# A mixture-of-experts block on one core: W2 loaded ahead of the last rows of W1, slot tables built among the first tiles, merged rank sums, eight products for the W2 row sums, no unread products, and the last ten tile words loaded by SyncE

## The reference

```python
x = x + xattn(ctx, ctx, layernorm(x), Wk, Wv, bv, Wq, bq, Wo, bo)   # 16 x 256 tokens of 128, 64 keys for each batch
t = layernorm(x)                                                    # 4096 tokens
p = softmax(t @ Wr + br)                                            # 8 experts
probs, idx = top_k(p, 2); probs = probs / probs.sum(-1)
h = layernorm(relu(t @ W1[e] + b1[e])) * g1[e] + be1[e]             # 128 -> 512, for each expert
y = layernorm(relu(h @ W2[e] + b2[e])) * g2[e] + be2[e]             # 512 -> 128
out = x + sum over the token's two experts of gate * y
```

## Time and profile before

| | |
|---|---|
| runs, median (range) | 316.07 us (314.22 to 317.29) |
| profiled execution, and its span | 314.07 us, 312.4 us |
| TensorE matmul, weight load | 251.5 us (81%), 196.5 us (63%) |
| VectorE, ScalarE, GpSimd | 227.6 (73%), 208.3 (67%), 189.3 us (61%) |
| mean granted TensorE clock | 0.885 of full |
| DMA | 34.46 MB, mean 110 GB/s |

### The profile page before, as it was taken

The page is one execution under the profiler, slowest core; times in us unless marked ns, Lnnn a source line. Parts: engine busy times, 40 slices in busy tenths (PEclk is TensorE's granted clock), DMA queues, the critical chain, the costliest instruction groups (busy, mean ns, idle before and its releaser), DMA issues.

```text
span 312.4 us, 8770 instructions
## 1 busy us (share of the span) xinstructions
PE 251.5 (81%) x2605; PEld 196.5 (63%) x2605; DVE 227.6 (73%) x1091; ACT 208.3 (67%) x795; POOL 189.3 (61%) x298
## 2 busy tenths in 40 slices
PE   2998629795929292746997998999999999899895
PEld 2465427454728171314896887798989987899531
DVE  1687918560359366738796778798989898899875
ACT  2557517734636294672796769698989898799920
POOL 8403545572634536364746786768888887788750
PEclk9998958877857667585998999999999999999999
DMA  6995672210411131243533123223232459551347
GB/s 183 342 286 173 199 238 62 76 43 28 135 35 60 59 104 52 59 100 87 113 65 75 47 62 81 61 68 70 72 72 45 129 131 196 138 137 46 96 146 241
DMA packets 48667, 34.46 MB, mean 110 GB/s; under 512 B 26871, under 2 KB 42743, under 8 KB 48620
## 3 DMA queue, kind: packets, MB, share of 16 engines
q1 hardware_dynamic: 38972, 22.80, 27.5%
q0 software_dynamic: 6592, 9.00, 9.9%
q10 hardware_dynamic: 3056, 2.11, 2.2%
HBM read 15.11 MB, written 12.02 MB: 87 GB/s over the span
## 4 chain that ended last, share of the span: by engine, by line
PE 35%; DVE 32%; another core or an unknown queue 14%; ACT 10%; issue 6%; DVEq 1%; DMA 1%; ACTq 0%
PE bank L720 20%; PE bank L724 13%; DVE kq L1884 5%; DVE cxT L1900 3%; DVE cx L1915 3%; DVE st L1905 2%; DVE hl L1884 2%; DVE w2f L1651 2%; ACT ex L1179 2%; ACT xt L1202 1%; DVE rs L1924 1%; ACT w1l L1221 1%; DMA wr<-in_L_ffn_Wr 1%; DVEq L1896 1%
## 5 line engine op out<-in xcount | busy, mean ns | idle before, releaser
L664 POOL DMA_INDIRECT slot_rows<-pay,pos x64 | 64.8, 1013 | 62.8 <-DVE pay L1757 45.7
L724 PE MATMUL bank<-w2h,kq 128*128 x384 | 59.1, 222 | 4.7 <-DVE cxT L1900 3.8
L720 PE MATMUL bank<-kb_room,w1h 128*128 128x128 f16 x568 | 57.4, 223 | 1.3 <-issue 0.9
L720 PE MATMUL bank<-kb_room,w1l 128*128 128x128 f16 x284 | 52.9, 223 | 0.5 <-issue 0.5
L678 POOL DMA_INDIRECT answers<-vo,words_of x36 | 35.5, 987 | 19.7 <-ACT vo L1383 10.9
L720 PEld LDWEIGHTS bank<-kb_room,w1h 128*128 x568 | 43.5, 100 | 6.0 <-issue 4.5
L678 POOL DMA_INDIRECT answers<-cx,words_of x35 | 34.6, 988 | 14.0 <-issue 8.2
L724 PEld LDWEIGHTS bank<-w2h,kq 128*128 128x128 f16 x384 | 37.7, 99 | 7.7 <-ACT kq L1349 5.6
L704 POOL DMA_DIRECT2D words_of<-slot_rows x71 | 40.7, 575 | 2.6 <-issue 2.3
L724 PE MATMUL bank<-kq 128*128 128x256 f16 x192 | 37.7, 276 | 0.8 <-DVE kq L1884 0.8
L1884 DVE SCALAR_TENSOR_TENSOR kq<-bank,kq 128x512 f16<-128x512 f32 x48 | 32.7, 682 | 0.4 <-ACT kq L1349 0.4
(11 more groups left out here) (265 smaller groups left out, 700.0 us busy)
## 6 DMA issues: line engine op xcount, KB each, us to landing
x_tok<-in_x SPq DMA_DIRECT2D x8, 256.0 KB, 7.2
w1f<-in_L_ffn_W SPq DMA_DIRECT2D x2, 1024.0 KB, 9.0
pay<-pay SPq DMA_DIRECT2D x8, 256.0 KB
w1f<-answers SPq DMA_DIRECT2D x8, 256.0 KB
w2f<-answers SPq DMA_DIRECT2D x8, 256.0 KB, 3.0
kb_room<-slot_rows SPq DMA_TRANSPOSE x71
words_of<-slot_rows POOLq DMA_DIRECT2D x71, 1.0 KB
w2l<-in_L_ffn_W SPq DMA_DIRECT2D x4, 256.0 KB, 11.2
```

The costliest lines, as they stand in the source:

```text
L664: eng.indirect_dma_start(slot_words, bass.IndirectOffsetOnAxis(ap=pos[:, g % 2, k, i:i + 1], axis=0), pay[g % 2][:, k, i, :].bitcast(U32), ...
L720: return eng.matmul(dst, lhsT, rhs, start=start, stop=stop)
L724: return eng.matmul(dst, lhsT, rhs, start=start, stop=False, skip_group_check=True)
```

## The change

1. SyncE issues both halves of W2 right after both halves of W1, then the eight broadcast rows `w1_last`. b1, the zero rows and g2 come behind the first payload copy.
2. `keep` is gone: 71 products of 256 columns.
3. `ranks(g)` now also carries the sums on; `base_next` and `rows_next` are gone; counts come from the same sums (`rows_so_far`, `rows_held`).
4. `w_rows`: 4 products of 512 columns with 8 stationary columns per half instead of 16 of 128 columns with 2. The first part of half 0 moves from the end of turn 3 to the end of turn 2.
5. Square sums of W2 in turns 1 and 2 instead of 2 and 3; those of W1 partly in the middle of turn 4.
6. In turn 8 `down_low(2)` and `up(0)` stand ahead of `ranks(7)`, `up(1)` right behind.
7. `gates`, `rest_places`, `words(1)`, `shares_` move from ahead of the tile loop into tiles 0 to 7.
8. be2 terms of groups 0 and 1 in 8 products of 128 columns, at every third tile from 28; the four transposes of the shares at tiles 16 to 22 instead of all at 16.
9. The words of tiles 61 to 70 are loaded by SyncE, not GpSimd. `back_at` moves from 52 to 68 to 58 to 70. `with_x` moves into the last two turns of the loop. `FIRST_BY_PE` is `(2,)`.
10. Some 30 waits that other waits imply are dropped.

```diff
-        offsets_at = {SHARE_AT + 4 + 2 * g: g for g in range(2)}
+        LATER, SHARE_AT = 5, 16
+        turned_at = {SHARE_AT + 2 * n: n for n in range(GROUPS // 2)}
+        quarters_at = {SHARE_AT + 12 + 3 * n: n for n in range(2 * GT)}
-        FIRST_BY_PE = (2, 3, 4)
+        FIRST_BY_PE = (2,)
...
+            for h in range(2):
+                eng.dma_start(w2f[:, h * H * FC:(h + 1) * H * FC, :],
+                              A["L0_ffn_W2"][h * H:(h + 1) * H].rearrange("e (c p) d -> p (e c) d", p=P)
+                              ).then_inc(ld_w2[h], 16)
...
+            def late_words(j):
+
+                eng.wait_ge(s_ans[(j - NW) % NZ], answered(j - NW))
+                if j >= LATE + GROUPS:
+                    eng.wait_ge(s_rg, j - GROUPS + 1)
+                eng.dma_start(words_of[:, j % NW, :], slot_words[bass.ds(place_of[j], P), D:]
+                              ).then_inc(ld_x[(j - LATE) % GROUPS], 16)
...
-            def keep(n):
-
-                for _ in range(n):
-                    mm(bank[2][:, 2 * P:], ones_b[:, 0:P], ones_b)
...
             def ranks(g):
-                m = mask[g % 2]
+                here = g * GT * E
+                if g > 0:
+                    eng.wait_ge(s_pos, g)
+                    mm_beside(base, not_below[:, :], mask[:, here - GT * E:here])
                 eng.wait_ge(s_mask, g + 1)
-                mm_beside(base, below[:, :], m[:, :])
+                mm_beside(base, below[:, :], mask[:, here:here + GT * E])
+                mm_beside(rows_so_far, onesb[:, :], mask[:, here:here + E])
...
-                for n in range(first + part * H * FC // 2, first + (part + 1) * H * FC // 2):
-                    t = mm(bank[6 + h][0:2, at_d:at_d + D], gm[:, n, :], w2f[:, n, :], False,
-                           n % (H * FC) == H * FC - 1)
+                for c in range(part * FC // 2, (part + 1) * FC // 2):
+                    t = mm(bank[6 + h][0:E, :], gm[:, h * FC + c, :], unit_in(w2_flat, h * FC + c), False, c == FC - 1)
...
+            def offset_quarter(n):
+
+                g, i = n // GT, n % GT
+                if n == 0:
+                    eng.wait_ge(ld_be2, 16 * 2 * GT)
+                    eng.wait_ge(s_shareT, 1)
+                of, at = slice(g * GT * E, (g + 1) * GT * E), slice(i * D, (i + 1) * D)
+                mm(psX[g][:, at], partsT[of, 0:P], be2_diag[of, at]).then_inc(p_off, 1)
...
                 if p == 0:
-                    eng.wait_ge(s_tab, 2)
-                    regs = pack_regs(eng, 0, PACKS)
-                    shares_()
+                    eng.wait_ge(s_tab, 1)
+                    regs = pack_regs(eng, 0, W_PACKS)
+                    gates()
...
+                if 1 <= p < 5:
+                    rest_places(2 * p - 2)
+                    rest_places(2 * p - 1)
+                if p == LATER + 1:
+                    words(1)
+                    shares_()
```

More of the change, by code:

```diff
@@ L186, in build @@
         oh = sb("oh", [P, GROUPS, K, GT, E])
-        mask = [sb(f"mask{n}", [P, GT * E], BF16) for n in range(2)]
+        mask = sb("mask", [P, TILES * E], BF16)
         pick = sb("pick", [P, K, GT * E])
@@ L349, in build @@
         ld_ctx = [signal(f"ld_ctx{h}") for h in range(2)]
-        ld_x = [signal(f"ld_x{g}") for g in range(GROUPS)]
+        ld_x = [signal(f"ld_x{g}_late_words{g}") for g in range(GROUPS)]
         ld_w1 = [signal(f"ld_w1_{h}") for h in range(2)]
@@ L575, in sync @@
                 tile_rows(j)
+                if j - BEHIND >= LATE:
+                    late_words(j - BEHIND)
                 if j in back_at:
                     answers_back(back_at[j])
+            for j in range(SLOT_TILES - BEHIND, SLOT_TILES):
+                late_words(j)
             for g in range(GROUPS - 2, GROUPS):
@@ L707, in gpsimd @@
                 words(j)
+            for i in range(GT):
+                payload_out(GROUPS - 1, 0, i)
             for p in range(SLOT_TILES + 4):
@@ new lines, in chunk, with addresses @@
+            def chunk(t, j, c, n=P):
+                return t[c][:, bass.ds(off[j], n)]
+            def addresses(j):
+                e_ = (regs[j // PACK] >> (BITS * (j % PACK) + P.bit_length() - 1)) & (E - 1)
+                off[j] = eng.snap(e_ * WS, min_val=0, max_val=(E - 1) * WS)
+                for c in range(FC):
+                    for t in (w1h, w1l):
+                        eng.lower_ap(chunk(t, j, c), for_matmul_weights=True)
+                    eng.lower_ap(chunk(w2h, j, c, P + 1))
+                    eng.lower_ap(chunk(w2l, j, c))
@@ new lines, in offset_sums @@
+            def offset_sums(g):
+                if g < 5:
+                    eng.wait_ge(s_rl, SLOT_TILES - 4 + g)
+                else:
+                    eng.wait_ge(s_u, SLOT_TILES - 7 + g)
+                to = offset_bank(g)[:, :]
+                of = slice(g % 2 * GT * E, (g % 2 + 1) * GT * E)
+                t = mm(to, partsT[of, g // 2 * P:(g // 2 + 1) * P], be2_diag[of, :], True, False)
+                t = mm(to, ident[:, :], group(x2, g)[:, :, 0:D], False, g not in FIRST_BY_PE)
+                if g in FIRST_BY_PE:
+                    eng.wait_ge(s_back[g], 16 * K * (GROUPS - 2))
+                    t = mm(to, ident[:, :], ya[g][0], False, True)
+                t.then_inc(p_off, 1)
@@ L1115, in tensor @@
                 down_lo(p)
[L1116 to L1119 removed]
+                if p == LATER:
+                    places(1)
+                if p == LATER + 2:
+                    eng.wait_ge(s_tab, 2)
+                    regs += pack_regs(eng, W_PACKS, PACKS)
+                if p in turned_at:
+                    shares_turned(turned_at[p])
+                if p in quarters_at:
+                    offset_quarter(quarters_at[p])
             for g in range(2, GROUPS):
@@ L1232, in w_rows_copy @@
                 eng.wait_ge(p_rows, h + 1)
-                copy(half(w2_rows, h), bank[6 + h][0:2, :]).then_inc(s_rows_, 1)
+                copy(half(w2_rows, h), bank[6 + h][0:E, :]).then_inc(s_rows_, 1)
             def c2_scaled():
@@ L1924, in roots, with with_x @@
                 eng.reciprocal(rs[p % 4][:, :], sd[p % 4][:, :]).then_inc(s_rs, 1)
+            res = Count(q_res)
+            at = {}
+            def with_x(g):
+                eng.wait_ge(p_off, offsets_done(g))
+                xg = group(x2, g)[:, :, 0:D]
+                res.up(eng.tensor_tensor(xg, offset_bank(g)[:, :].rearrange("p (i d) -> p i d", i=GT), xg, ALU.add))
+                at[g] = res.n
             for p in range(SLOT_TILES + LAG2):
```

375 lines of the change are left out of this document (145 added, 230 removed).

## The result

The changed kernel takes 303.66 us, the median of 6 runs (301.62 to 306.22), against 316.18 us before. The ratio is 0.959, with a 95% interval of 0.954 to 0.964. The forecast was 311.0, in a range of 301.5 to 318.0: the time lies inside the range and the direction is right, but the gain is 12.5 us where 5 were forecast, 2.5 times as large. It landed 0.7 us above rival B (301 to 303 us).

A forecast was written before the change was run, and what follows sets the result against it. First stage bound by scatter bursts, late releases and the group chain; second by 1.79 us tiles. Terms -1.1 -1.5 +0 -3.0 +2.5 +1 -0.3 -1.3 = -3.7 gave 310.4 or 312.4; it took 311.0, range 301.5 to 318.

The forecast's parts named there:

- rival B: First stage: without `keep` ahead of `probT`, two or three more groups' transposes end before the burst; -9, 301 to 303; chance 0.18.
- Loads: W2 issued right behind W1 is there early, taking 1.1 us off the first scatter burst; bounds 0 and 2.
- keep: First stage: without five products ahead of `probT` and `ranks`, two groups gain 0.65 us and one 0.15; 1.5 us, bounds 0 and 5.
- Merged ranks: First stage: carried sums move from ahead of the group into its chain, one 8-column product more; 0.1 us, left out.
- Most transposes end well inside the burst: First stage: argument that two or three more groups would not get their transposes done before the scatter burst takes hold.
- `w_rows`: Same 2048 columns streamed in fewer products: 0; half of half 0 a turn earlier: 0, bounds -3.5 and +3.5.
- Fewer instructions: In `w_rows`, 4 products of 512 columns replace 16: 0, or -1 if the instruction count matters.
- Start of the second stage: VectorE from the last count to `r_lo(0)`: gates, tables, words and waits leave; -3.0, bounds 1.6 to 3.4.
- In-loop tables and clock: Tables, words and shares moved into the tile loop: +2.5 (0 to 3.2); first tiles may meet the lower clock: +1 (0 to 2.5).
- Tail: Two float32 products of 1.02 us less on TensorE, two more adds on VectorE, two `with_x` leave; -1.3, bounds 0 and -2.
- C: Tile loop: the 3.0 us earlier start is taken back by stalls and tables; then -1, 313 to 315; chance 0.20.
- D: Without `keep`, TensorE stays at 0.50 in the first stage; +3.3, 317 from the profiled execution, 319 from the median; chance 0.12.

The follow-up runs named there:

- quick condition: State seen in the follow-up job where no TensorE or VectorE signal rose over 0.8 us late in the first stage; the unchanged kernel took 269.54 us.
- second job: The change, the old kernel without `keep`, and two tail edits of the change, beside the old kernel at 317.14 us; change 303.34 (0.955), without `keep` 313.18 (0.986).
- first job: Old kernel (269.54 us) without `keep` 270.68, with one float32 product per `keep` 269.86, 16-column `keep` 273.93; changed kernel with `keep` back 262.07. Also called the quick job.

## Why the prediction was wrong in its size

*Loads: -1.1 forecast, +0.2 measured.* The first scatter starts at 33.45 us, no earlier: it waits for the group's chain, not for W2. In my sum the release of the earlier trace rows at 45.02 was put down in part to transfers. The kernel with `keep` and `base_next` changed, whose loads stand as before, has a first gap of 13.6 us against 13.3: the loads gave at most 0.3 there.

*keep: -1.5 forecast, -1.5 measured* in the gaps when taken alone, in one profile; 4 us in the median of the whole, whose interval is 2 to 7. The product count that goes with it is in the next point.

*Merged ranks: 0.1, "left out". This is the step that failed.* I priced the move of `base_next` by TensorE's time and found none. It took 8 products from between a group's first scatter and its transposes. Together with `keep`'s 5 that is worth about 10 us of the gaps (110.8 to 100.5) and 8.7 us of the median, where my two terms had 1.5. In the prediction I had seen that the release "comes near the end of a burst" and had asked only how early in a burst the transposes end; rival B carried that idea, with 0.7 to 1.3 us of `keep` as its means. B came within 0.7 us, and its mechanism did not come true. The transposes of the changed kernel end 4.4 and 2.3 us earlier in the burst in groups 2 and 3, but within 0.7 us of the old place in groups 0, 4 and 5, and these are on time as well, behind 22, 10 and 5 records instead of 32, 38 and 18. So B's number was luck. "Most transposes end well inside the burst" was my argument against B, and it is void, since being inside the burst does no harm by itself. The sign that I had named, that I would be wrong if the number of late releases changes, is what the trace shows. I had also read the releases a little off: the copies start 2.6 to 2.8 us after the eighth scatter starts, in four groups, not 3 to 4 in three.

*`w_rows`: 0, +-3.5.* Same columns, and rightly the same time: at the higher clock a part takes 1.91 us in 16 records before and 1.88 us in four after. But its records were 32 of the 46, 16 of the 39 and 16 of the 38 ahead of the transposes in groups 2, 3 and 4. "Fewer instructions" was given a bound of 1 us; it names the right quantity, and what it is worth here was not isolated. The part that moved did land ahead of another group's transposes, as the forecast feared:

```profile
53.31 3.55 PE L752 MATMUL bank<-w2f,gm 128*8 128x512 f32 x4
```

With the product ahead of them these keep TensorE busy from 51.51 to 56.86, in group 1. VectorE has that group's probabilities ready at 50.33 and the transposes start at 56.79. Gap 1 is the only one that got longer, 15.1 us against 13.5.

*Start of the second stage: -3.0 forecast, -2.8 measured* (4.6 us from the eighth burst to `r_lo(0)`, now 1.8).

*In-loop tables and clock: +2.5 and +1.* The first ten turns have 5.9 us over 1.79 a turn, before 3.8; in the quick condition 3.3 against 0.9. That is +2.1 and +2.4. The granted clock over the first 20 us of the loop is 0.86, where the earlier trace rows had 1.00 from 149 us on:

```profile
133.00:153.00 20.00, 18.49 (x233) 16.59 (x234) 16.37 (x69) 11.14 (x45) 10.98 (x14) 0.86 0.43 102
```

Both together were to be 3.5 and are 2 to 2.5 in those turns. The whole loop lost 5.5 us in the first profile and 2.7 and 3.5 in two profiles of other jobs. The rest is spread over stalls of 0.3 to 2.5 us at 24 tiles instead of 16. In the quick condition the old kernel's loop has 8 or 9 of them. What the change adds there was not taken apart. In the prediction I had misread the old kernel's stalls as "1 to 3 us at some twelve tiles": 12 tiles have more than 0.5 us, 9 of them more than 1, and none more than 2.5.

*Tail: -1.3 forecast, -1.0 measured,* and +1.0 in the tail, +1.7 in the median, when the two products come back. TensorE's 13 products end at 296.7, but the end is now set by the answers' last load:

```profile
297.16 0.69 DVE L1957 TENSOR_TENSOR w2f<-bank,w2f 128x512 f32<-128x512 f32 x1 [0.53 <-DMA w2f<-answers]
```

*Rivals.* C: the loop gave back 2.3 us more than forecast in the first profile, and 0.3 more and 0.5 less in the two others. D, the clock, came true as far as the clock goes: 0.60 over 30 to 60 us in the changed kernel, 0.83 before. Its price did not show where signals are late: without `keep` alone the second job is faster, 0.986. Where none is late, it is 0.8%.

## What to carry to other kernels

When a consumer waits for a signal that came late without any work to explain it, count instructions, not microseconds: what the producer has issued since the burst of scattered DMA began. Look at each signal of the chain, and not only at the first that is late: here a later one, VectorE's own, holds the group once the transposes pass. Take products that nobody waits for out of that stretch, join small products into wide ones, or put them behind the signal that the chain needs, but not ahead of the next thing it needs. And measure a kernel like this in more than one job: the same program took 269.5 and 316 us, and a product that helps in the one harms in the other.

## What the runs showed of the hardware

- While GpSimd's eight scatters of a group are in flight, signals of TensorE can arrive up to 7.9 us after their product's recorded end, and signals of VectorE up to 4.1 us; no signal of ScalarE's rose more than 0.8 us late in the first stage of any trace. The signal of the transposes is on time behind 16 records of TensorE or fewer, and late behind 26 or more. For TensorE it cannot be told whether the signal is held or the product itself runs late, since the ends of matmuls are modelled.
- The same kernel, before, took 269.5 us in one job and 310.5 in another on the same chip. In the four traces of the first job, of other kernels than before itself, no signal was late in the first stage, the transposes' not even behind 47 records. The cause of the two conditions is open.
- The granted clock of a whole run was higher with products that nothing reads, in the quick job: 0.923 to 0.959 with them, 0.902 to 0.924 without. In the second job the ranges overlap, 0.872 to 0.896 and 0.869 to 0.884.
